# Eight PSUM banks shared out anew in a convolution layer: two pairs for the blocks, two banks each for turned and projected rows

## What is computed

```python
x = x + linear_attention(_gn(x), ...)        # layer 0, not touched by the change
# layer 1: 7x7 circular convolutions for each channel, a gate, a recurrence of 8 steps, a projection
gate_A = sigmoid(conv(x, gate_A_kernel));  gate_B = sigmoid(conv(x, gate_B_kernel))
b_t = conv(x, B_kernel) * gate_B;          a_t = conv(ones, A_kernel) * gate_A
h   = exp(scan(log sigmoid(-a_t), log sigmoid(a_t) + log(softplus(b_t) + 1e-6), 8 steps))
x = x + h @ W_out + b_out
```

## Time and profile before

| | |
|---|---|
| median of 3 runs | 6414.13 us (6409.31 to 6427.77) |
| the profiled execution | 6436.69 us, its span 6434.9 us |
| busy over the span | PE 87%, PEld 80%, DVE 67%, ACT 61%, POOL 65% |
| DMA over the span | 1439.13 MB, mean 224 GB/s |
| layer 1 | from 3516.4 us to the end |
| mean granted TensorE clock | 0.956 of full speed |

### The profile page before, as it was taken

How to read it: one execution, slowest core, us unless ns; L and a number is a source line. 1 busy time by engine, 2 the same in 40 slices (tenths; PEclk the granted TensorE clock), 3 DMA queues, 4 the chain that set the end, 5 groups by cost and what they waited for, 6 DMA issues and landing times. The chain is left out here.

```text
span 6434.9 us, 131484 instructions
## 1 busy us (share of the span) xinstructions
PE 5598.9 (87%) x51252; PEld 5148.7 (80%) x51252; DVE 4312.7 (67%) x5123; ACT 3940.2 (61%) x5128; POOL 4181.0 (65%) x3608
## 2 busy tenths in 40 slices
PE   6789999999999999999972688888888888888887
PEld 5578888888888888888862578887788888887787
DVE  6367777777767777777745966676666777666653
ACT  5677777777777777777522456565555555655554
POOL 0146676766676666767674967777677677777651
PEclk9899999999999999999985799999999999999999
DMA  5357777777777777777664599999999999999987
GB/s 130 131 158 224 225 224 222 225 223 219 226 227 223 222 223 224 220 223 225 180 177 129 144 248 261 255 264 251 247 257 258 267 268 264 265 259 262 247 239 212
DMA packets 1239104, 1439.13 MB, mean 224 GB/s; under 512 B 142960, under 2 KB 1025396, under 8 KB 1238516
## 3 DMA queue, kind: packets, MB, share of 16 engines
q1 hardware_dynamic: 1238516, 1431.07, 78.4%
HBM read 999.09 MB, written 431.64 MB: 222 GB/s over the span
## 5 line engine op out<-in xcount | busy, mean ns | idle before, releaser
L1231 PE MATMUL psC<-wide,xhl 128*128 128x256 bf16 x6144 | 1057.8, 283 | 55.6 <-DMA wide<-toeplitz_wide 42.9
L1228 PE MATMUL psC<-wide,xhl 128*128 128x192 bf16 x6144 | 877.5, 253 | 0.0
L1161 POOL TENSOR_TENSOR stage<-stage,nrow 128x1024 f32<-128x1024 f32 x240 | 621.9, 2591 | 375.9 <-DMA stage<-x_by_block_row 359.9
L1178 POOL COPY down<-xhl 48x448 f32<-48x448 f32 x512 | 526.1, 1028 | 470.7 <-PE psC L1237 371.7
L787 POOL TENSOR_TENSOR y<-y,grow 128x1024 f32<-128x1024 f32 x256 | 604.9, 2363 | 344.1 <-DVE y L654 344.1
L1322 ACT ACTIVATE xhl<-psC 128x512 f32<-128x512 f32 x512 | 303.2, 598 | 690.8 <-PE psC L1237 689.2
L1237 PE MATMUL psC<-narrow,down 128*128 128x96 bf16 x6144 | 539.4, 213 | 168.2 <-POOL down L1181 103.0
L1228 PEld LDWEIGHTS psC<-wide,xhl 128*128 128x128 bf16 x6144 | 646.8, 116 | 20.2
L1231 PEld LDWEIGHTS psC<-wide,xhl 128*128 128x128 bf16 x6144 | 597.9, 116 | 70.8 <-issue 53.8
L1429 DVE SCALAR_TENSOR_TENSOR xhl<-xhl,psC 128x512 f32<-128x512 f32 x512 | 347.2, 680 | 454.7 <-ACT xhl L1322 454.4
L1337 ACT ACTIVATE hT<-psH 128x512 f32<-128x512 f32 x512 | 304.6, 595 | 536.6 <-PE psH L1273 536.1
(11 more groups left out here) (167 smaller groups left out, 13786.8 us busy)
## 6 DMA issues: line engine op xcount, KB each, us to landing
wide<-toeplitz_wide SPq DMA_DIRECT2D x1024, 140.0 KB, 5.9
xa<-in_x SPq DMA_DIRECT2D x256, 512.0 KB, 4.7
xb<-in_x SPq DMA_DIRECT2D x256, 512.0 KB, 3.9
xc<-in_x SPq DMA_DIRECT2D x256, 512.0 KB, 5.7
x_rows<-xc SPq DMA_DIRECT2D x256, 512.0 KB
res<-x_rows SPq DMA_DIRECT2D x256, 512.0 KB, 9.4
out<-res SPq DMA_DIRECT2D x256, 512.0 KB, 8.4
stage<-x_by_block_row SPq DMA_DIRECT2D x225, 512.0 KB, 9.4
```

The source lines that it names most:

```text
L1161: nc.gpsimd.tensor_tensor(v, v, nrow[:, 0:1, :].to_broadcast([P, NP_, C]), ALU.mult).then_inc(s_scaled, 1)
L1178: nc.gpsimd.tensor_copy(dst[lo, :, :, 0:last], src[lo, :, 0:NQ, CW:])
L1228: nc.tensor.matmul(dst[:, :, :, 2:], lhs, tab[:, :, 32 + part * 12:44 + part * 12], start=False, stop=False)
L1231: nc.tensor.matmul(dst, lhs, tab[:, :, part * 16:part * 16 + 16], start=(n == 0), stop=False)
```

## The change

`CR` becomes 2, so `psC` holds two pairs (four banks), and `psH` and `psO` get two banks each (`OR` = 2), used in turn by the rows. The waits follow the rings: `conv_first` of block b now waits for the product of block b-2, `turn(t)` for `evacuate(t-2)`, `project(t)` for `add(t-2)`. The table `wide_before` stays for the DMA loads of the wide table, whose ring keeps three buffers. A short prelude that turned sixteen small windows through `psH`, `psO` and the third pair now goes through the four single banks. On every engine the same instructions stand in the same order as before.

```diff
-    WR, NR, DR, CR = 3, 2, 2, 3
+    WR, NR, DR, CR, OR = 3, 2, 2, 2, 2
...
         psC = [ps(f"psC{k}", [P, CB, 2, P]) for k in range(CR)]
-        psH = ps("psH", [C, HS, P])
-        psO = ps("psO", [P, HS * C])
+        psH = [ps(f"psH{k}", [C, HS, P]) for k in range(OR)]
+        psO = [ps(f"psO{k}", [P, HS * C]) for k in range(OR)]
...
         def psT(k):
-            return (psH[:], psO[:].rearrange("p (s c) -> p s c", c=C),
-                    psC[2][:, 0:2].rearrange("p c v m -> p (c v) m"),
-                    psC[2][:, 2:4].rearrange("p c v m -> p (c v) m"))[k]
+            return (psH[0][:], psO[0][:].rearrange("p (s c) -> p s c", c=C),
+                    psH[1][:], psO[1][:].rearrange("p (s c) -> p s c", c=C))[k]
...
             def conv_first(img, par, blk):
-                count = img * NBLK + wide_before(blk) + 1
+                count = img * NBLK + blk - CR + 1
                 if known(count):
                     pe.wait_ge(s_prod, count)
...
             def turn(oi, par, t):
-                count = oi * HR + t
+                count = oi * HR + t - OR + 1
                 if known(count):
                     pe.wait_ge(ht_evac, count)
-                    mm = nc.tensor.transpose(psH[:, s, :], hv[:, :, t * HS + s], ident[:])
+                    mm = nc.tensor.transpose(psH[t % OR][:, s, :], hv[:, :, t * HS + s], ident[:])
...
             def project(oi, t):
-                count = oi * HR + t
+                count = oi * HR + t - OR + 1
                 if known(count):
                     pe.wait_ge(s_added, count)
-                nc.tensor.matmul(psO[:].rearrange("p (s c) -> p s c", c=C), ones3[:],
+                nc.tensor.matmul(psO[t % OR][:].rearrange("p (s c) -> p s c", c=C), ones3[:],
                                  bias_k[:].to_broadcast([P, HS, C]), start=True, stop=False)
```

More of the change, by code:

```diff
@@ L1279, in project @@
                     pe.wait_ge(s_fixed, oi * NFIX + fixes(t))
-                count = oi * HR + t
+                count = oi * HR + t - OR + 1
                 if known(count):
                     pe.wait_ge(s_added, count)
-                nc.tensor.matmul(psO[:].rearrange("p (s c) -> p s c", c=C), ones3[:],
+                nc.tensor.matmul(psO[t % OR][:].rearrange("p (s c) -> p s c", c=C), ones3[:],
                                  bias_k[:].to_broadcast([P, HS, C]), start=True, stop=False)
                 for s in range(HS):
-                    mm = nc.tensor.matmul(psO[:, s * C:(s + 1) * C], hT[:, t % 2, s * P:(s + 1) * P], w[:],
+                    mm = nc.tensor.matmul(psO[t % OR][:, s * C:(s + 1) * C], hT[:, t % 2, s * P:(s + 1) * P], w[:],
                                           start=False, stop=(s == HS - 1))
@@ L1336, in evacuate @@
                     act.wait_ge(o_ready, count)
-                nc.scalar.activation(hT[:, t % 2, :], psH[:].rearrange("p s m -> p (s m)"), ACT.Copy,
+                nc.scalar.activation(hT[:, t % 2, :], psH[t % OR][:].rearrange("p s m -> p (s m)"), ACT.Copy,
                                      bias=A_FREE * H_EPS, scale=A_FREE).then_inc(ht_evac, 1)
@@ L1489, in add @@
                 part = res[:, k, (t % 2) * HS * C:(t % 2 + 1) * HS * C]
-                nc.vector.tensor_tensor(part, psO[:], part, ALU.add).then_inc(s_added, 1)
+                nc.vector.tensor_tensor(part, psO[t % OR][:], part, ALU.add).then_inc(s_added, 1)
             def image(img, par, has_conv, has_out, has_stage):
```

## The result

The changed kernel takes 6349.57 us (median of 6 runs, 6340.83 to 6376.72) against 6415.41 us (6 runs, 6403.55 to 6427.77) before: ratio 0.9903, 95% interval 0.9886 to 0.992. That is 1.0% faster, 65.8 us. The forecast was 27 us off with a range down to 6305 us: the direction and the range held, the size was 2.4 times too small. The time fell where my first rival stood with half of its waits kept (some 6350 us). The profiled execution took 6350.71 us with a span of 6348.9 us. Against the span before (6434.9 us) that is 86 us; the profiled execution before was itself 21 us above its median.

The account below looks back on a forecast made before the run. DMA was taken as the nearer bound in the middle of an image, TensorE close behind. Middles 21 + last image 4 + flush 9.6 - seams 7.5 = 27 us off 6414.1, giving 6387 us; 8-in-10 range 6305 to 6438.

Parts of the forecast that it names:

- my first rival: Loosened waits stay saved, DMA being no limit: 125 us off, 6289 us; with half kept, some 6350 us; chance 0.17.
- The step that failed: In layer 1 only TensorE's waits for the addition (84.3 us) and the copy (47.8) are loosened, together 132.1 us; others stay.
- the last rival: Seam gets dearer: clock falls at block 31, 3 us an image, 45 in all, giving 6449 us; chance 0.18.
- DMA as the nearer bound: Mid-image, blocks 5 to 26: DMA at share 1.03 is nearer its bound than TensorE, which idles about 16 of 128.8 us.
- the middle's term: Middles of 14 images: most saved waits return as waits for tables or `down`; 1.5 us gained an image, 21 us.
- The signs that I named: Among them: middle at 127 us, share 1.03 or more; `narrow` and `down` waits grown by most of 119 us.
- The seam's cost: Around image ends, late products of block b-2 cost 0 to 1.8 us an image; 0.5 taken, 7.5 us over 15 images.
- The stall at block 31: Block 31 begins 2.9 us late, waiting for block 29's product, covered by TensorE's 3.71 us wait before the next image.
- the slower rival: Clock falls after idling before block 31, whose 3.2 us become 5.2; run slower at 6449 us; chance 0.18.
- Block 3's stall: Block 3 waits 2.7 us for block 1's product, covered by the first turn's softplus wait of 3.62 us; cost nothing.
- The last image and the flush: Last image keeps about half of its 7.9 us, 4 us; flush gains 0.31 us a row over 31 rows, 9.6 us.

## Why the prediction was right or wrong, point by point

**The step that failed** is the first: the change loosens two of TensorE's waits, 132.1 us, and "the others (…; the edge correction, 72.3; …) stay". The 72.3 us were the addition's under another name, as the runs without corrections and with two banks for projected rows alone show. So 204 us were loosened. That matters most at the seams, the term that was furthest off: I had given them no gain at all and a cost of 7.5 us, and they gave 27.2. In each of the 13 seams one such wait stood at block 27, 31.4 us in all, 2.4 each, and it went. The seams' waits for the softplus (49.4 us to 10.0) and for the narrow table (17.8 to 0.2) shrank too; against them came the product (47.3) and `down` (2.0 to 35.4). Left over are the 14.4 us of idle time.

**A term put at nothing.** The sum priced waits alone, and of the clock only its fall in the last rival. TensorE's busy time at the same matmuls fell by 41 of the 86.6 us, and no term of the sum stood for it. I had also written that the trace shows the low clock at the seam alone. That was misread: 0.97 in the middle of image 6 means low stretches there too.

**DMA as the nearer bound** was wrong for the kernel before, and this was the mechanism on which the middle's term rested. Its share of 1.03 with tables landing after 8.7 us looked like a limit, and taking away 18% of the traffic changed nothing. That the middle's term still came out near (21 us forecast, 32.6 in the profiled pair) is in part luck. The waits came back as forecast, because the change made that bound real: in the 14 middles the addition, the misnamed waits and the copy went from 150 us to 1, `down` and `narrow` from 83 to 215. The idle time kept was 14.1 us, less than the 21; the other 18.5 are busy time, which I had not counted. The signs that I named were there: the middle stood at 126.7 us (127 forecast) with a share of 1.03. After the change less traffic does give time. The Trainium skill ("Perfetto Trace Analysis", "Identifying the Most-Contended Engine") says that the busy share of the DMA engines misleads, as there are 16 of them, and that the use of HBM should be taken instead. The kernel before agrees on the share: 275 GB/s at 1.03 and 221 GB/s at 0.80 gave the same middle. But the changed kernel has the same share and nearly the same rate, 280 GB/s, and there less traffic does shorten the middle; here neither number told the two kernels apart. For the first rival I had also weighed the Trainium skill's limit of HBM, some 358 GB/s for a core ("DMA: Bandwidth & Descriptors", "Where 436 GB/s comes from"); the highest rate of the stretches shown here is 301.

**The seam's cost.** The stall at block 31 came as worked out and was covered. The changed kernel at the same place (image 5, TensorE):

```profile
4571.08 0.52 PE L1230 MATMUL psC<-wide,xhl 128*128 128x256 bf16 x3 [2.75 <-DVE xhl L1428]
...
4572.65 0.84 PE L1230 MATMUL psC<-wide,xhl 128*128 128x256 bf16 x3
...
4575.37 0.69 PE L1230 MATMUL psC<-wide,xhl 128*128 128x256 bf16 x3
```

2.75 us were lost (2.9 forecast), and half of the slower rival happened too: from 4572.65 the same three matmuls take 0.84 us and not 0.49, the clock having fallen to 1.2 GHz after the idle time. The next image's block 0 followed at once, at 4575.37. What was late next is what I had named, the wide table of block 1: TensorE began that block at 4581.27, after a wait of 2.73 us for it. From where block 31 could have begun (4568.33) that is 12.9 us; before it was 13.4 (4595.43 to 4608.78). With the two pairs alone the 13 seams took 623.7 us against 622.1, and the ratio was 1.0007, so my 7.5 us lie inside its interval and cannot be told from nothing. Block 3's stall was covered by the softplus wait, as said.

**The last image and the flush** were right in kind and too small. The image gave 10.7 us, not 4: its idle time shrank by 3.9, as forecast, and the other 6.8 are busy time at a clock of 1.00 in place of 0.96. The rest to the end gave 16.1, not 9.6, 13.0 of it idle time. I had capped a row of the flush at 1.83 us by DMA, that is at 1.17 times 245 GB/s, 287. A row took 1.54 us at first and 1.70 in the mean (31 steps from the first row at 6289.36 to the last at 6342.20), since now and then an addition waited for the load of its `res`:

```profile
6327.07 1.29 DVE L1489 TENSOR_TENSOR res<-psO,res 128x512 f32<-128x512 f32 x2 [2.84 <-DMA res<-x_rows]
```

Over 40 us of the flush the engines passed 301 GB/s at a share of 0.94:

```profile
6300.00:6340.00 40.00, 37.62 (x309) 35.61 (x308) 15.68 (x28) 14.21 (x24) 0.00 (x0) 1.00 0.94 301
```

**The second bank of turned rows** I had counted with 47.8 us of the gain; by itself it is worth nothing or less.

## What to carry to other kernels

A wait for several semaphores was named here after the event nearest in time. Before one calls such a wait untouched, one looks at which row or buffer the named instruction belongs to: here the correction named was that of the next row, and the real releaser ended 0.1 us before it. A DMA share of 1 and long landings can stand beside a bound that lies elsewhere; less traffic at the same work is the test. Where two banks are to be given away, each ring is tried by itself: here one bank for the projected rows, whose additions stand behind long operations in VectorE's queue, was the whole gain. And a difference is split into idle and busy time of the engine that bounds: nearly half of this one, in the profiled pair, was the same matmuls in less time at a higher clock.

## What the runs showed of the hardware

A DMA share near 1 is no fixed rate: 275 to 280 GB/s at 1.03 in the middle of image 6, 301 at 0.94 in the flush after, which moves `res` and `out` alone. A narrow table of 168 KB landed 7.2 us after its issue at full traffic and 3.4 us after it at 18% less.

TensorE's clock fell to 1.2 GHz within 1.6 us of the engine's going on after an idle time of 2.75 us at block 31, while it had stayed up after one of 2.28 us at block 15 of image 6 in the kernel before.

A VectorE operation of 0.17 us lasted 2.22 us while POOL was in an operation of 2.38 us, and ended with it.
